# A two-layer graph attention kernel: adjacency and x handed over with columns and features on the partitions, and 48 of 64 mask units made by GpSimd

## The reference

```python
# layer 0: 8 heads of 128
Wh = einsum('nf,hfd->hnd', x, W_heads)
s1 = einsum('hnd,hd->hn', Wh, a1); s2 = einsum('hnd,hd->hn', Wh, a2)
e = s1[:, :, None] + s2[:, None, :]
e = where(e > 0, e, 0.2 * e)
e = where(adj[None] > 0, e, -9e15)
hp = elu(einsum('hnm,hmd->hnd', softmax(e, -1), Wh))
x = layernorm(x + hp.transpose(1, 0, 2).reshape(N, 1024) @ W_out + b_out)
# layer 1: 4 heads of 64, same adjacency, no W_out
x = layernorm(x + gat(x, adj, W, a))
```

## Time and profile before

| | us |
|---|---|
| median of 3 runs | 2611.09 |
| lowest and highest | 2610.91, 2614.13 |
| span of the profiled execution | 2610.2 |
| TensorE busy | 2572.1 |
| VectorE busy | 2112.9 |
| ScalarE busy | 2129.2 |
| GpSimd busy | 108.7 |

### The profile page before, as it was taken

One profiled execution on the slowest core, in us unless ns is written; L12 is line 12 of the kernel. 1 busy time (PEld: TensorE's weight loads), 2 busy tenths in 40 slices (PEclk: granted clock), 3 DMA queues, 4 the chain that ended last, 5 costly groups with the idle time before them and its releaser, 6 DMA issues.

```text
span 2610.2 us, 62540 instructions
## 1 busy us (share of the span) xinstructions
PE 2572.1 (99%) x25977; PEld 2293.6 (88%) x25977; DVE 2112.9 (81%) x4336; ACT 2129.2 (82%) x3318; POOL 108.7 (4%) x151
## 2 busy tenths in 40 slices
PE   9999999999999999999999999999999999999998
PEld 6578888888888888888888888888888889999998
DVE  5468888888888888877878878788755689999998
ACT  5478888888888888888888888888873579999997
POOL 1220000000000000000000000000002520000000
PEclk9999999999999999999999999999999999999999
DMA  8965424243342533321211111221225655333340
GB/s 296 327 217 134 124 67 121 67 108 106 83 120 69 124 88 84 110 74 46 63 43 52 52 49 44 57 60 36 48 70 187 230 209 201 109 114 105 134 126 20
DMA packets 324115, 285.01 MB, mean 109 GB/s; under 512 B 124661, under 2 KB 268024, under 8 KB 323834
## 3 DMA queue, kind: packets, MB, share of 16 engines
q1 hardware_dynamic: 285130, 243.54, 32.2%
q10 hardware_dynamic: 38704, 37.49, 4.5%
HBM read 195.13 MB, written 57.74 MB: 97 GB/s over the span
## 4 chain that ended last, share of the span: by engine, by line
PE 84%; ACT 7%; DVE 5%; issue 1%; DMA 1%; ACTq 0%; DVEq 0%
PE l_ps L913 69%; PE l_ps L1003 7%; ACT l_arena L1245 6%; PE l_ps L933 4%; PE l_ps L885 2%; DVE l_arena L1738 1%; PE l_ps L952 1%; DVE l_arena L1735 1%; DMA l_wh<-l_arena 1%; DVE l_arena L1763 1%; DVE l_arena L1761 0%; DVE l_arena L1722 0%; PE l_ps L944 0%; DVE l_arena L1772 0%; DVE l_arena L1782 0%
## 5 line engine op out<-in xcount | busy, mean ns | idle before, releaser
L913 PE MATMUL l_ps<-l_arena 128*128 128x258 f16 x16384 | 1802.4, 273 | 0.6 <-ACT l_arena L1113 0.6
L913 PEld LDWEIGHTS l_ps<-l_arena 128*128 128x128 fp8e4 x16384 | 1603.0, 98 | 200.3 <-ACT l_arena L1113 1.2
L1141 ACT ACTIVATE l_arena<-l_arena 128x512 fp8e4<-128x512 f32 x2048 | 1282.1, 709 | 78.3 <-PE l_ps L913 76.4
L1533 DVE SCALAR_TENSOR_TENSOR l_arena<-l_arena,l_mask 128x512 uint32<-128x512 uint32 x512 | 354.8, 693 | 202.6 <-ACT l_arena L1141 200.2
L1245 ACT ACTIVATE l_arena<-l_arena 128x1024 fp8e4<-128x1024 f32 x443 | 465.3, 1137 | 14.4 <-PE l_ps L1003 14.1
L1003 PE MATMUL l_ps<-l_arena 128*128 128x130 f16 x8000 | 459.3, 221 | 16.8 <-DVE l_arena L1738 12.0
L1003 PEld LDWEIGHTS l_ps<-l_arena 128*128 128x128 fp8e4 x8000 | 455.9, 98 | 20.1 <-DVE l_arena L1738 14.7
L1534 DVE TENSOR_TENSOR l_arena<-l_arena,l_mask 128x512 uint32<-128x512 uint32 x512 | 355.0, 693 | 0.0
L1513 DVE SCALAR_TENSOR_TENSOR l_arena<-l_arena 128x129 f16<-128x129 f32 x960 | 274.5, 349 | 8.4
L1176 ACT COPY l_arena<-l_ps 128x258 f32<-128x258 f32 x256 | 94.2, 368 | 218.3 <-PE l_ps L913 218.3
L1539 DVE SCALAR_TENSOR_TENSOR l_arena<-l_ps,l_arena 128x258 f32<-128x258 f32 x256 | 116.6, 483 | 114.2 <-ACT l_arena L1176 114.1
(11 more groups left out here) (170 smaller groups left out, 1166.1 us busy)
## 6 DMA issues: line engine op xcount, KB each, us to landing
l_arena<-in_adj SPq DMA_DIRECT2D x38, 1024.0 KB, 6.1
l_arena<-uv SPq DMA_DIRECT2D x125, 272.0 KB, 5.3
l_arena<-l_wh SPq DMA_DIRECT2D x120, 256.0 KB, 4.9
l_arena<-in_adj ACTq DMA_DIRECT2D x20, 1024.0 KB, 7.5
l_arena<-l_srow SPq DMA_DIRECT2D x64, 256.0 KB, 3.3
l_arena<-feat SPq DMA_DIRECT2D x32, 512.0 KB, 3.8
feat<-l_arena ACTq DMA_DIRECT2D x63, 256.0 KB, 2.4
l_wh<-l_arena SPq DMA_DIRECT2D x64, 192.0 KB, 5.7
```

Source lines behind the costliest of these rows:

```text
L913: last = nc.tensor.matmul(sums(t, m), pattern(k, m).bitcast(F8)[:, j, t * P:(t + 1) * P], uv[:, slot(v, order[k]) + j, m * WH:m * WH + 2 * ...
L1141: ins = act.activation(pattern(k, 0).bitcast(F8)[:, j, :], s1b[q][:, :], ACT.Relu, bias=kc[:, h, jt:jt + 1], scale=STEEP, saturate=False)
L1533: dve.scalar_tensor_tensor(c, v, ONE8X4, m, ALU.bitwise_xor, ALU.bitwise_and)
```

## The change

The host hands over three arrays in another order. `x_columns` is x with features on the partitions, loaded in four parts straight into `xt`; the turns of x are gone. The adjacency comes as 64 units `adj_units` [128 columns, 2048], one for each block and chunk in the order in which the sweeps use them: a unit is 4 column tiles x 512 rows, columns on the partitions. W has its rows on the partitions. a1 and a2 are broadcast by DMA, on ScalarE's queue with the weights.

A mask unit is now one operation, raw int32 greater than zero to fp8. VectorE makes units 0 to 15 (`make_mask`, at steps 16 to 96); GpSimd makes units 16 to 63, 16 to 31 as soon as they are loaded behind `make(7)` and unit 15, then 4 in each round. Units 0 to 19 are loaded ahead of the sweeps (3 by SP at the start behind unit 0, 16 by ScalarE), 20 to 31 by SP into three places in the mask. `FRONT` is 12 instead of 6, product i waits for copy i - 7 in place of i - 3 (seven banks), product i of the first x parts for their loads, all eight `make(c)` lie ahead of the sweeps.

```diff
-    UNITS, EARLY, WIDE, HALFWAY = NB * CPB, 24, 24, HB * CPB
-    first_turns = [(0, 3), (0, 5), (0, 7), (1, 1), (1, 5), (1, 7), (2, 0), (2, 1)]
+    UNITS, EARLY, HOMES, HALFWAY = NB * CPB, 16, 20, HB * CPB
+    first_turns = [(0, 1), (0, 2), (0, 3), (0, 4), (0, 5), (0, 7), (1, 1), (1, 4), (1, 5), (1, 6), (1, 7),
+                   (2, 0), (2, 1), (2, 2), (2, 5), (2, 6)]
     late_turns = [(0, 5), (1, 1), (1, 5), (2, 1)]
-    FRONT, FAR = 6, 10
+    FRONT, FAR = 12, 10
+    unit_at = [16 + n * 80 // (EARLY - 1) for n in range(EARLY)]
+    made_at = {SCORED + 16 + 4 * c: c for c in range(CPB)}
+    xparts = [(0, 2), (2, 6), (6, 16), (16, NT)]
+    rotation = [0, 1, 2, 4, 5, 6, 7]
...
+            def make_mask(n):          # GpSimd
+                pool.wait_ge(s_ul[home(n)], loads(n))
+                if n == EARLY:
+                    pool.wait_ge(s_md, EARLY)
+                else:
+                    pool.wait_ge(s_mp, n - EARLY)
...
+                nc.gpsimd.tensor_scalar(unit_mask(n).bitcast(U8), raw(n), 0.0, float(ONE8), ALU.is_gt, ALU.mult).then_inc(s_mp, 1)
+
             for c in range(CPB):
                 make(c)
+            for n in range(EARLY, UNITS):
+                make_mask(n)
...
             def load_unit(n):          # SP
...
+                if n >= HALFWAY:
+                    sp.wait_ge(s_mp, n - EARLY)
+                    sp.wait_ge(s_pe, HC * round_of(n))
+                elif n >= HOMES:
                     sp.wait_ge(s_pw, STEPS)
...
+                    if n >= HOMES + 3:
+                        sp.wait_ge(s_mp, n - 2 - EARLY)
...
+            load_x(0)
+            load_x(1)
+            load_x(2)
             load_unit(0)
+            load_x(3)
+            for n in range(1, 4):
+                load_unit(n)
             for i in range(STEPS):
...
                 store_step(i)
...
                 for m in range(CPB):
-                    if (g, m) in packed_in:
-                        n = packed_in[g, m]
-                        cross_unit(n)
+                    if (g, m) in made_in:
+                        n = made_in[g, m]
+                        if HOMES <= n < HALFWAY - 3:
                             load_unit(n + 3)
                         elif n >= HALFWAY and n % PER < PER - 1:
                             load_unit(n + 1)
...
             def product(i):            # TensorE
-                if i > 2:
-                    pe.wait_ge(s_cw, i - 2)
+                if i >= len(rotation):
+                    pe.wait_ge(s_cw, i - len(rotation) + 1)
...
+            def make_mask(n):          # VectorE
                 dve.wait_ge(s_ul[home(n)], loads(n))
...
+                dve.tensor_scalar(unit_mask(n), raw(n), 0.0, None, ALU.is_gt, saturate=False).then_inc(s_md, 1)
...
-                    if (g, m) in packed_in:
-                        pack_late(packed_in[g, m])
```

More of the change, by code:

```diff
@@ L119, in network @@
     STEPS, NW, SCORED = len(steps), 6, FRONT + NT
-    spent = [sum((parts[q][1] - parts[q][0]) * D for q, _ in steps[:i]) for i in range(STEPS)]
-    packed_at = [next(i for i in range(STEPS) if (spent[i] - spent[7]) * (EARLY - 1) >= n * (spent[86] - spent[7]))
-                 for n in range(EARLY)]
-    turned_at = [i + 3 for i in packed_at]
-    made_at = {56: 0, 60: 1, 64: 2, 68: 3, 90: 4, 97: 5}
-    XPARTS = 4
+    unit_at = [16 + n * 80 // (EARLY - 1) for n in range(EARLY)]
+    made_at = {SCORED + 16 + 4 * c: c for c in range(CPB)}
+    xparts = [(0, 2), (2, 6), (6, 16), (16, NT)]
+    firsts = [first for first, _ in xparts]
+    rotation = [0, 1, 2, 4, 5, 6, 7]
     dram = lambda name, *shape: nc.dram_tensor(name, shape, F32).ap()
@@ L164, in network @@
         words = uv[:, :, :].rearrange("p c w -> p (c w)").bitcast(I32)
[L165 to L167 removed]
+        twin, RAW = CPB * JC * WH, 4 * blk
         far = mask_t[:, :, :].bitcast(F32)
@@ L213, in network @@
         s_ac, s_mg = (s.sem(n) for n in ("ac", "mg"))
-        s_ml = [s.sem(f"ml{r}") for r in range(2)]
         K = feat.shape[1]
@@ L301, in landed @@
         def landed(t):
-            return 16 * [arrival(u) for u in range(t + 1)].count(arrival(t)) + (16 if arrival(t) == 0 else 0)
+            return 16 * [arrival(u) for u in range(t + 1)].count(arrival(t))
         def last_use(t):
@@ L352, in packed @@
-        def packed(n):
-            if in_mask(n):
-                return mask_t[:, 28 + n % 2, HB * blk:NB * blk]
-            first = slot(round_of(n) + 1, 2) * WH if n >= HALFWAY else 0
-            return (packs[n % 2] if n < HALFWAY else words[:, first:first + PK]).bitcast(U8)
-        def raw(n, k):
-            return landing(n)[:, k]
-        def pair(n, k):
-            if in_mask(n):
-                return packed(n).rearrange("p (h j k) -> p h j k", h=2, k=2).bitcast(F8)[:, :, :, k]
-            return packed(n).rearrange("p (j k) -> p j k", k=2).bitcast(F8)[:, :, k]
@@ L366, in corner, with raw @@
-        def corner(n):
-            return n // CPB * blk + n % 2 * 2 * P, n % CPB // 2 * 2 * JC
-        def unit_bank(n):
-            return banks[4 + n % 4]
+        def raw(n):
+            h = home(n)
+            if n >= HALFWAY or h < 2:
+                first = slot(round_of(n) + 1, 3) * WH if n >= HALFWAY else twin + h * RAW
+                return words[:, first:first + RAW].rearrange("p (j k i) -> p j k i", j=JC, k=2)
+            if h < 4:
+                rows = mask_t[:, 8 * h:8 * h + 8, 2 * blk:HB * blk].bitcast(I32)
+                return rows.rearrange("p (j k) i -> p j k i", k=2)
+            first = 16 + 4 * (h - 4)
+            return mask_t[:, first:first + JC, HB * blk:NB * blk].bitcast(I32).rearrange("p j (k i) -> p j k i", k=2)
@@ L714, in _ @@
                         load_mean(g)
-            for n in range(EARLY, EARLY + 2):
+            for n in range(HOMES, HOMES + 3):
                 load_unit(n)
@@ L1294, in _ @@
                     act.activation(sc[:, :, :], tb, ACT.Exp).then_inc(s_ex, 1)
-                for n in range(4, EARLY):
-                    if packed_at[n - 4] + 2 == i:
+                for n in range(4, HOMES):
+                    if unit_at[n - 4] + 2 == i:
                         load_unit(n)
-                for n in range(EARLY):
-                    if packed_at[n] == i:
-                        pack(n)
                 if i in (85, 93):
@@ L1825, in _ @@
                 for n in range(EARLY):
-                    if packed_at[n] == i:
-                        pack(n)
-                for n in range(EARLY):
-                    if turned_at[n] == i:
-                        write_mask(n)
+                    if unit_at[n] == i:
+                        make_mask(n)
                 if i in (8, 12, 16, 20):
@@ L1852, in _ @@
                     split(gk, k)
-                    if g == 0 and m in (0, 2):
-                        make(6 + m // 2)
                     if m == 1 and g > 0:
```

274 lines of the change are left out of this document (69 added, 205 removed).

## The result

The changed kernel is slower: 2725.94 us median (2720.6 to 2734.45) against 2612.2 us, ratio 1.0439 with a 95% interval of 1.0417 to 1.0461. The profiled execution has a span of 2728.1 us, 117.9 more than before. I had forecast 2624 us (2594 to 2662): the sign was right, the size was not. In the code after, line 824 is the sweep matmul (913 before), 807 the products (885), 1022 ScalarE's comparison, 1390 and 1391 the split (1533, 1534), 1366 and 1369 make_next, 1396 to 1421 evacuation and division, 473 GpSimd's mask.

What follows compares the result with a forecast made beforehand. TensorE, busy 99%, was taken to bound the kernel, so only time ahead of the first sweep can be gained. -17 (start) + 12 (first four sweeps) + 18 (masks 32 to 63) = +13 us, 2624 us, range 2594 to 2662.

Steps and rivals of the forecast that it cites:

- ahead of the first sweep: Stretch before the first attention sweep: it starts at 140 us instead of 157.1, 17 us gained (11 to 23).
- The wait for store 0: Ahead of the first sweep: copy 6 needs store 0's slot, store 0 lands behind the loads, so product 13 starts at 34 us.
- What the mask costs on GpSimd: One GpSimd mask of 2048 elements, priced nearest to a cast: 2.3 us, ends 1.9 and 3.7 (4.2 with narrow output).
- Rival B: GpSimd needs 3 us or more a mask: -17 + 25 + 35 = +43 us, 2654 us; chance 0.2.
- Who waits for it: In the sweeps: each GpSimd mask blocks VectorE's next two-input instruction for up to the mask's time, taken as 2.3 us.
- T: Time of one GpSimd mask, taken as 2.3 us.
- First four sweeps: Masks 16 to 31 hold VectorE longer than its room in the first four sweeps: plus 12 us (3 to 30).
- masks 32 to 63: Four masks a round over eight rounds, landing just ahead of a sweep's last split: plus 18 us (2 to 40).
- the sign of being wrong that I had named: Gaps ahead of first chunks would mean that evacuation, not the last split, is tight.
- rival A: Blocking is absorbed, a mask takes 1.9 us or less: -17 + 3 + 2 = -12 us, 2599 us; chance 0.32.
- the late mask as a rival: Masks too late for their sweeps: dropped, as mask 31 is due about 105 us into the sweeps; no chance given.
- A to D: Four outcomes: A 2599 us (0.32), B 2654 (0.2), C head start mostly lost 2611 (0.14), D the forecast 2610 to 2640 (0.34).

Runs made afterwards that it cites:

- loads_later: The changed kernel with all masks on VectorE, and unit loads 0 to 3 moved behind products 5, 8, 11 and 14 in SyncE's queue: 2601.68 us, ratio 0.9964.
- the quarters: The changed kernel with each GpSimd mask cut into four instructions of 512 elements: 2635.57 us, ratio 1.0095.
- The cast: The changed kernel with GpSimd's masks made by one cast from int32 to fp8 in place of compare and multiply: 2620.28 us, ratio 1.0033.
- the halves: The changed kernel with each GpSimd mask cut into two instructions of 1024 elements: 2623.15 us, ratio 1.0047.

## Why the prediction was wrong

**What bounds the kernel, and ahead of the first sweep.** That a change can gain only ahead of the first sweep and lose wherever a sweep waits held: -13.0 us ahead, all loss in the sweeps, none behind unit 63, layer 1 unchanged (458.6 us of matmuls, 459.3 before). I gave 140 us for the first sweep (134 to 146), it was 144.13. The term that was off is when the weights land: 29.28 us, not 17. ScalarE's queue took 11.18 us to issue four weight loads (my price was 3.36 us for four), in the same time in which SyncE's took 11.26 us for one unit load. So product 12 waited for the weight scores until 39.46, not 28. The wait for store 0 came as predicted, copy 6 at 34.98 against my 34, but it was over before product 12 began. That store 0 lands behind the loads thus held, and *loads_later* shows it from the other side (copy 6 at 23.5). The Trainium skill (DMA: Bandwidth & Descriptors, Queues, rings and completion order) says less than I took from it: descriptors of one queue start in order, but a later one may finish its write before an earlier one. Part of the wait was no matter of that order at all, since SyncE was still issuing loads until 22.4 us and issued store 0 only then. The sum did not hang on it after all.

**What the mask costs on GpSimd.** This is the first step that failed, and the largest. I bounded it by 1.9 and 3.7 us (4.2), took 2.3, and it is 7.08. My nearest row was a cast, and a cast of the same unit does cost 1.89. I chose the row by operand count and width, as if GpSimd paid by the elements it moves. The runs show 1.89, 5.37 or 7.08 us for one input of 2048 elements, by the form of the operation. Rival B named the fear (two operations an element) but priced it within the same bounds. The estimate from the Trainium skill, 3.1 us (GPSIMD Engine Reference, Performance versus the Vector engine), is nearer and still under half.

**Who waits for it.** Right in kind: VectorE is kept out while GpSimd works, and the trace of before showed it. Wrong in measure: I let each mask block the next two-input instruction for up to T. A two-input instruction lost 4.3 us beside 7.08, a one-input one all of it, and the evacuation and division chain has both, one behind another. I had read the Trainium skill (SBUF — State Buffer, Who interferes with whom) too coarsely: it says that an instruction in a two-port mode and one of GpSimd exclude each other for the whole instruction, while one with two SBUF inputs contends only with GpSimd's reads. The rows above the step agree (7.07 us for the one-input instruction, 4.72 for the two-input one); that the latter gets in when GpSimd has read would fit that account, but is argued here and not shown. The rows below the step don't agree with the first half: 1.03 us for the one-input instruction beside a 1024-element mask that takes 3.63.

**First four sweeps, and masks 32 to 63.** With T at 2.3 I had 12 and 18 us; they were 39.8 and 56 us. That the late hits would be of a few us and end by sweep 35 was right. The place was not: this is the second step that failed. I had the last split as the tight one, 0.8 us ahead, and priced masks 32 to 63 by hits there. Of their 56 us, 28 stand ahead of chunk 2 and 21 ahead of chunk 3, whose splits come behind division and make_next in VectorE's queue, and 6 ahead of chunks 6 and 7. That is near the sign of being wrong that I had named, gaps ahead of first chunks. With short holds the last splits are the tight ones indeed: in the quarters all ten gaps behind the fourth sweep, of 0.2 to 0.7 us, are ahead of chunks 6 and 7. The cast is the nearest test of the sum at a T within my bounds: 1.89 us, 13.9 us of gaps and 2620 us, where I had 2599 (rival A) at 1.9 and 2624 at 2.3. At its own T the sum was 21 us too low. That 2620 lies near my 2624 is partly luck, since the start was 4 us worse than in the sum and 7 us of matmul time had no term. Had the mask been a cast, the time would have been within my range, but not by the right terms.

**Supply.** I dropped the late mask as a rival since 16 masks of under 6 us make it, and said that load_block and cross are late only above 5 us. At 7.24 us a mask or more, and next to no break from 133.7 to 254.5 us, that condition was met, and cross was what suffered, as the halves show.

**The clock.** The sum held no term for it. TensorE had full clock throughout before, so no row gave a price; in the changed kernel 36.1 us, a third of the loss, is matmul time, nearly all behind 17 gaps of 2.3 us and more, with the granted clock at 0.50 for some microseconds. The cast, whose gaps are short, shows 7 us, 3.0 of them behind its one gap of 3.40 us.

**Rivals.** None of A to D has the time. B has the condition (3 us or more a mask) and names the form; its +43 us was +114. Against its 25 and 35 us of hits stand 39.8 and 56, and 36 of clock for which it had nothing. My range ended just above B's middle because T was taken as bounded by rows of other forms.

## What to carry to other kernels

Before work is moved to GpSimd, find a row of that very form (operation, both operands) on it, or time it alone; a row of a cast says nothing of a compare. Try GpSimd instructions beside VectorE at 1024 elements a partition or fewer, and prefer VectorE at 1.22 us to GpSimd at 7.08 if it has the room. A wait put ahead of a load in a shared queue delays everything behind it in that queue, and a gap on TensorE costs its length and, in most cases here, the slower matmuls behind it.

## What the runs showed of the hardware that I had not expected

- GpSimd, 128x2048, alone: compare then multiply 7.08 us, compare or multiply alone 5.37, multiply-add in f32 1.90, copy or cast 1.89.
- A mask instruction of GpSimd (compare then multiply) kept a two-input VectorE instruction out for 0.41 us (512 elements) to 0.84 us (1024) although it ran on for 1.92 to 3.63 us, and at 1088 elements the one-input instruction took 1.09 us in all. From 1152 elements on it kept a one-input instruction out to its end, and a two-input one for 3.5 to 4.3 us. A copy kept the one-input instruction out for its whole length at 1024, 1280 and 2048 elements. Where the step comes from, and whether it goes by elements or bytes, is open.
- GpSimd waits in turn: masks that take 7.08 us alone took up to 10.7 us beside VectorE.
- A gap of 2.40 us on TensorE was followed by matmuls at a granted clock of 0.50 (1.2 GHz); another of 2.41 us was followed by matmuls at 1.00. Of 21 gaps of 2.2 us and more, 17 cost 1.5 to 3.1 us of matmul time and four cost 0.2.
